# Vision tower on one core: the complex attention of the first half of the batch runs alone, the second half's runs under the first half's norms and first layer

## What is computed

```python
h = tokens(x)                                      # (8, 66, 192)
h = h + complex_attention(layernorm(h))
h = h + tower(layernorm(h))                        # 4 layers, RMS norms ln1, ln2, final

def complex_attention(x):                          # 12 heads of 16
    qr, qi, kr, ki, v = (heads(x @ W.T) for W in (Wqr, Wqi, Wkr, Wki, Wv))
    sr = (qr @ kr.T + qi @ ki.T) / 4
    si = (qi @ kr.T - qr @ ki.T) / 4
    return softmax(sqrt(sr * sr + si * si)) @ v

# one layer of the tower
nx = rms(h, ln1[i])
h = h + softmax(q @ k.T + bias) @ v @ attn_o[i]    # q, k, v = nx @ attn_q, attn_k, attn_v
nx = rms(h, ln2[i])
h = h + relu(nx @ ffn_wi[i]) @ ffn_wo[i]           # + experts in layers 1 and 3
```

## Time and profile before

| | us |
|---|---|
| runs | 795.41, 798.39, 814.34 |
| median of the runs | 798.39 |
| the profiled execution | 800.37 |
| its span from first to last instruction | 798.6 |

### The profile page before, as it was taken

One profiled execution on the slowest core, in us unless ns is written; L12 is line 12 of the kernel. 1 busy time (PEld: TensorE's weight loads), 2 busy tenths in 40 slices (PEclk: granted clock), 3 DMA queues, 4 the chain that ended last, 5 costly groups with the idle time before them and its releaser, 6 DMA issues.

```text
span 798.6 us, 16388 instructions
## 1 busy us (share of the span) xinstructions
PE 733.1 (92%) x6735; PEld 649.1 (81%) x6735; DVE 438.8 (55%) x917; ACT 406.8 (51%) x913; POOL 352.6 (44%) x327
## 2 busy tenths in 40 slices
PE   6887999998998989899999999989999899999995
PEld 4764577776877979899999887768779788999995
DVE  0338435365364484566666634753555845766664
ACT  1467335535354353377777355353553545766642
POOL 3346516463663440155766332536544413355420
PEclk9976899998998898999999999989999999999997
DMA  7221001021311201053445020012212011523300
GB/s 203 80 70 41 2 2 31 9 73 41 99 41 31 70 2 56 1 163 111 138 128 145 13 75 1 2 40 74 68 31 70 6 51 53 143 71 108 101 1 22
DMA packets 36610, 49.21 MB, mean 62 GB/s; under 512 B 6155, under 2 KB 27575, under 8 KB 36023
## 3 DMA queue, kind: packets, MB, share of 16 engines
q1 hardware_dynamic: 33259, 43.49, 18.8%
q10 hardware_dynamic: 3276, 4.67, 1.9%
HBM read 47.70 MB, written 0.45 MB: 60 GB/s over the span
## 4 chain that ended last, share of the span: by engine, by line
PE 65%; DVE 12%; ACT 11%; POOL 6%; issue 3%; DMA 2%; SPq 0%; POOLq 0%; ACTq 0%; DVEq 0%
PE pd L653 35%; PE pa L653 19%; PE ps L653 8%; POOL w L582 3%; PE pa L684 3%; ACT wide L1015 2%; POOL prob L591 1%; DVE prob L1208 1%; ACT pa L1016 1%; DVE rc L1060 1%; ACT wqkv L927 1%; DVE xn L1095 1%; DVE xs L1067 1%; DVE hT L1135 1%; DVE mx L1055 1%
## 5 line engine op out<-in xcount | busy, mean ns | idle before, releaser
L582 POOL TENSOR_TENSOR w<-raw,w 128x384 fp32r<-128x384 f32 x140 | 142.7, 1021 | 124.6 <-ACT w L927 116.7
L653 PE MATMUL pd<-wide,w 128*128 128x264 f32 x1200 | 159.7, 291 | 0.0
L653 PEld LDWEIGHTS pd<-wide,w 128*128 128x128 f32 x1200 | 153.6, 194 | 1.0 <-DVE wide L1231 0.5
L653 PE MATMUL pa<-xs,w 128*128 128x264 f32 x810 | 123.4, 293 | 10.5 <-DVE wide L1231 6.2
L653 PEld LDWEIGHTS pa<-xs,w 128*128 128x128 f32 x810 | 108.7, 193 | 16.0 <-DVE wide L1231 8.2
L591 POOL TENSOR_TENSOR prob<-prob,mx 66x792 f32<-66x792 f32 x36 | 54.9, 1528 | 75.4 <-DVE mx L1055 75.2
L1231 DVE TENSOR_TENSOR wide<-pa,wide 128x264 fp32r<-128x264 f32 x144 | 61.4, 430 | 33.6 <-ACT pa L1016 31.7
L653 PE MATMUL ps<-xs,w 128*128 128x264 f32 x480 | 74.4, 285 | 3.1 <-DVE prob L1208 3.1
L1015 ACT ACTIVATE wide<-pa 128x264 fp32r<-128x264 f32 x144 | 56.7, 394 | 33.3 <-PE pa L653 33.2
L597 POOL TENSOR_TENSOR prob<-prob,rc 66x792 f32<-66x792 f32 x36 | 54.3, 1509 | 36.7 <-DVE rc L1061 36.7
L603 POOL TENSOR_TENSOR rs<-var,exponent 88x3 f32<-88x3 f32 x22 | 18.6, 848 | 115.5 <-DVE var L1077 115.5
(11 more groups left out here) (125 smaller groups left out, 1240.7 us busy)
## 6 DMA issues: line engine op xcount, KB each, us to landing
raw<-in_moe_w_dram SPq DMA_DIRECT2D x16, 576.0 KB, 4.2
raw<-in_moe_w_dram SPq DMA_DIRECT2D x16, 384.0 KB, 3.5
raw<-in_moe_w_dram SPq DMA_DIRECT2D x32, 192.0 KB, 4.0
vtok<-cw_rows ACTq DMA_DIRECT2D x4, 1056.0 KB, 6.1
raw<-in_attn_o_dram SPq DMA_DIRECT2D x4, 576.0 KB, 4.0
raw<-in_ffn_wo_dram SPq DMA_DIRECT2D x4, 576.0 KB, 4.1
vtok<-in_patches_dram SPq DMA_DIRECT2D x2, 768.0 KB, 7.9
raw<-in_attn_q_dram SPq DMA_DIRECT2D x4, 384.0 KB, 3.6
```

Of the source, the lines that this page charges most:

```text
L582: ins = nc.gpsimd.tensor_tensor(low, whole, high.bitcast(F32), ALU.subtract)
L653: return nc.tensor.matmul(out_ap, lhsT, rhs, start=first, stop=last)
```

## The change

1. The list is written anew from the first `cproj` to the first `pv`. The weights q and k are split before and between the first half's projections. The first half's scores follow without the second half's projections between them, and its roots stand one by one between them. The second half's projections come after the first half's exponentials, its scores and roots under the first half's norms, and its exponentials, transposes, values and norms between the scores and values of layer 0 of the first half. `pv` of the first half's images 0 and 1 is drawn ahead of the second half's `qk`. The `warm` entries are placed anew: 41 matmuls stand from the first `cproj` to the second half's first `qk` where there were 77.
2. `croot` is a stage for one image instead of four, and `qk` a stage for q or k instead of both. What each computes is as before.
3. DVE's wait for the `ps` banks in `cscores` is counted from the list, since scores of layer 0 no longer come after all complex scores.

Everything from `o_tail` of layer 0 on is as it was.

```diff
@@ stages() @@
-    for part in range(3):
-        yield ("cproj", 0, part)
-        if part == 0:
-            yield ("scale", 1, "complex", 0)
     yield ("split", None, "qkv", 0, 0)
+    yield ("cproj", 0, 0)
+    yield ("scale", 1, "complex", 0)
     yield ("split", None, "qkv", 0, 1)
...
+    yield ("cscores", 0, 3)
+    yield ("croot", 0, 2)
+    yield ("croot", 0, 3)
+    yield ("cvals", 0)
+    yield ("cvals", 1)
...
+    yield ("cscores", 1, 3)
+    yield ("croot", 1, 0)
     yield ("norm", 0, "ln1", 0)
+    yield ("croot", 1, 1)
...
+                yield ("pv", 0, 0, 0)
+                yield ("scores_end", 0, 0)
                 yield ("split", None, "o", 0, 0)
+                yield ("scale", 1, "ln1", 0)
+                yield ("pv", 0, 0, 1)
+                yield from warm(6)
+                early = 2
...
@@ pool: croot @@
-                    for b in range(HALF_B):
-                        sub_max()
+                    sub_max()
@@ tensor: qk @@
-                    for i in range(2):
-                        pe.wait_ge(chunk_split, chunks_until("qkv", layer, i))
-                        for m in range(KT):
-                            product(bank_a()[:, 0:NT],
+                    if i == 0:
+                        pe.wait_ge(x_ready, x_ready_after(("scale", hf, "ln1", layer)))
+                        flush()
+                    pe.wait_ge(chunk_split, chunks_until("qkv", layer, i))
+                    for m in range(KT):
+                        product(bank_a()[:, 0:NT],
@@ scalar: croot @@
-                    for b in range(HALF_B):
-                        u = hf * HALF_B + b
-                        act.wait_ge(csq_free, 2 * (u + 1))
+                    u = hf * HALF_B + stage[2]
+                    act.wait_ge(csq_free, 2 * (u + 1))
@@ vector: cscores, croot @@
-                            dve.wait_ge(s_free, 2 * (u + 1))
+                            dve.wait_ge(s_free, groups_after(S_GROUPS, stage))
...
-                    for b in range(HALF_B):
-                        u = maxes.next() - 1
-                        dve.wait_ge(sqrt_ready, u + 1)
-                        max_of(u)
+                    u = maxes.next() - 1
+                    dve.wait_ge(sqrt_ready, u + 1)
+                    max_of(u)
```

More of the change, by code:

```diff
@@ L126, in stages @@
[L126 to L142, removed]
+    yield ("cexp", 0, 3)
+    yield ("cproj", 1, 0)
@@ new lines, in stages @@
+    yield from warm(12)
+    yield ("cproj", 1, 1)
+    yield ("ctp", 0, 0)
+    yield ("cproj", 1, 2)
+    yield ("cpv", 0, 0)
+    yield ("ctp", 0, 1)
+    yield from warm(3)
+    yield ("cpv", 0, 1)
+    yield ("ctp", 0, 2)
+    yield from warm(3)
+    yield ("cpv", 0, 2)
+    yield ("ctp", 0, 3)
+    yield ("split", None, "qkv", 0, 2)
+    yield from warm(3)
+    yield ("cpv", 0, 3)
+    yield ("cscores", 1, 0)
+    yield ("mean", 0, "encoder")
+    yield ("cscores", 1, 1)
+    yield ("squares", 0, "encoder")
@@ L143, in stages @@
+    yield ("norm", 0, "encoder", 0)
+    yield ("cscores", 1, 2)
+    yield from warm(2)
     yield ("scale", 0, "encoder", 0)
     yield ("squares", 0, "ln1")
-    yield from warm(2)
-    yield ("ctp", 1, 2)
-    yield from warm(2)
+    yield ("cscores", 1, 3)
+    yield ("croot", 1, 0)
     yield ("norm", 0, "ln1", 0)
[L149 to L153, removed]
-    yield ("scale", 0, "ln1", 0)
-    yield from warm(2)
@@ L161, in stages @@
         if layer not in MOE_LAYERS:
-            yield from warm(4)
-            yield ("qk", 0, layer)
             if layer == 0:
+                yield ("qk", 0, 0, 0)
+                yield ("cexp", 1, 2)
+                yield ("cexp", 1, 3)
+                yield ("qk", 0, 0, 1)
+                yield ("ctp", 1, 0)
+                yield ("scores", 0, 0, 0)
+                yield ("cpv", 1, 0)
+                yield ("ctp", 1, 1)
+                yield ("v", 0, 0, 0)
+                yield ("cpv", 1, 1)
@@ new lines, in stages @@
+                yield ("ctp", 1, 2)
+                yield ("scores", 0, 0, 1)
+                yield ("cpv", 1, 2)
+                yield ("ctp", 1, 3)
+                yield ("v", 0, 0, 1)
+                yield ("cpv", 1, 3)
+                yield ("mean", 1, "encoder")
+                yield ("scores", 0, 0, 2)
+                yield ("squares", 1, "encoder")
+                yield ("v", 0, 0, 2)
+                yield ("norm", 1, "encoder", 0)
+                yield ("scores", 0, 0, 3)
+                yield ("scale", 1, "encoder", 0)
@@ L165, in stages @@
+                yield ("squares", 1, "ln1")
+                yield ("v", 0, 0, 3)
+                yield ("norm", 1, "ln1", 0)
+                yield ("pv", 0, 0, 0)
+                yield ("scores_end", 0, 0)
                 yield ("split", None, "o", 0, 0)
-                yield ("mean", 1, "encoder")
-                yield ("squares", 1, "encoder")
-                beside = [[("norm", "encoder", 0)], [("scale", "encoder", 0), ("squares", "ln1")], [("norm", "ln1", 0)], [("scale", "ln1", 0)]]
-            else:
+                yield ("scale", 1, "ln1", 0)
@@ L170, in stages @@
+                yield ("pv", 0, 0, 1)
+                yield from warm(6)
+                early = 2
+            else:
+                yield from warm(4)
+                yield from qk(0, layer)
                 beside = [[("norm", "ln1", layer)], [("scale", "ln1", layer)], [], []]
-            for b in range(HALF_B):
[L172 to L176, removed]
@@ L177, in stages @@
-            yield ("qk", 1, layer)
+                for b in range(HALF_B):
+                    yield ("scores", 0, layer, b)
+                    for x in beside[b]:
+                        yield (x[0], 1) + x[1:]
+                    yield ("v", 0, layer, b)
+                yield from warm(6)
+                early = 0
+            yield from qk(1, layer)
             if layer == 0:
```

76 lines of the change are left out of this document (29 added, 47 removed).

## The result

The changed kernel takes 814.7 us in the median of four runs (813.0 to 816.2); the kernel before took 798.8 in the four beside them. The ratio on record is 1.0173 (the two medians give 1.020), with a 95% interval of 1.0132 to 1.0214: slower by 1.3 to 2.1%, where 0.8% faster was forecast. The profiled execution took 813.33 and spans 811.5, against 800.37 and 798.6.

What follows compares the result with a forecast made beforehand. The prediction took PE, busy 92% of the span, as the bound. Its stretches summed as 25.7 - 6.2 - 13.4 + 0.4 = 6.5 us earlier at `o_tail`, so 798.4 - 6.5 = 791.9 us, range 784 to 800.

Steps and rivals of the forecast that it cites:

- A: Stretch from 29.2 to the first half's fourth `cpv`: forecast to take 43.4 us, ending at 72.6 instead of 98.3.
- if the clock is back at about 53: Assumption for the first half's value products: the last three take 0.94 us each, ending at 56.4; range 55 to 58.
- B: Stretch from the first half's last `cpv` to its `qk`: forecast 23.2 us, 17.0 before, cutting the lead to 19.5.
- the wait behind the second half's root: First half's ln1 `var` and power queue behind the second half's image 0: 4.5 us given away.
- C: Stretch from the first half's `qk` to the second half's: forecast 42.3 us, 28.9 before, cutting the lead to 6.1.
- If the 2.7 us of idle time before 138.1 bring it down: Bound on PE's clock at the second half's `qk`: it could lose up to about 4 us, leaving a lead of 2.5.
- rival 3: Clock falls before the second half's `qk` (4 us), later waits 2 us longer, no lead left: 797.9 us; chance 0.15.
- D: Stretch from the second half's `qk` to `o_tail`: forecast 31.3 us, 31.7 before.
- PE arrives 3.5 too early: Before `o_tail`, PE waits 3.5 us for ACT's copies of `v` behind POOL's weight split, where it waited 1.2 before.
- the lead of 6.5: Forecast gain at `o_tail` summed over the four stretches: 6.5 us earlier than before, at 169.4.
- All that follows shifts by it: From `o_tail` on, unchanged work was to move by the 6.5 us gained, giving 791.9 us.
- Rival 2: PE leaves the sparse norm stretch at 1.2 GHz and following work runs at half rate: 806.9 us; chance 0.10.

Runs made afterwards that it cites:

- e14: e9 with the second half's first projection moved ahead of the first half's value products: 790.3 us, ratio 0.9851.
- e1: The changed kernel with the first half's ln1 norm moved ahead of the second half's first root: 811.4 us, ratio 1.0122.
- e3: The changed kernel with the split of w1 moved ahead of the second half's first `qk`: 802.0 us, ratio 0.9987.
- e8: The kernel before with the split of w1 moved ahead of the second half's `qk`: 799.3 us, ratio 0.9987.
- e2: The changed kernel with 32 more filler matmuls between and behind the first half's complex scores: 812.3 us, ratio 1.0138.
- e11: The changed kernel with 11 more `warm` around the encoder norm and 6 ahead of its second-half scale: 810.4 us, ratio 1.0108.
- e4: The kernel before with 37 `warm` put ahead of layer 0's `o_tail` as a pure delay: 809.4 us, ratio 1.0077.
- e12: The changed kernel measured again, unedited: 815.0 us, ratio 1.0174.
- e10: e9 with the filler around the first half's encoder norm added: 793.6 us, ratio 0.9881.
- e13: The kernel before with the early split of w1 and 36 more filler matmuls: 797.1 us, ratio 0.9955.
- e9: The changed kernel with e1, e2, e3 and e6 combined, filler placed ahead of the second half's norm scales, `pv` of image 1 moved back: 794.5 us, ratio 0.9894.
- e15: e9 measured again, unchanged: 794.0 us, ratio 0.9910.
- e6: The changed kernel with the second half's ln1 scale moved ahead of the first `pv` and layer 0's last sum: 812.4 us, ratio 1.0164.

## Why the prediction was wrong, step by step

**A, "if the clock is back at about 53": failed.** Of the 6.6 us, 4.1 are the clock's: the last five value products took 8.4 instead of 6.3, and the rest of the stretch 18.2 instead of 16.2. The clock's return was taken from the earlier trace rows, 9 and 11 us after PE took up work again; here it took 21 us (from 44.8 to 65.8, and 24 from the fall). The step had this as a point with a range of 2 us; its bounds were too narrow. (The prediction has the falls "some 1.5 to 2 us" after PE ran out of work; by the windows of the same trace it was 1.0 and 2.0, and 3.4 at the third.) The other 2.5 us are the later start of the fourth value product, and most of that a term that the sum left out: ACT's last root waited 1.51 for DVE's additions beside POOL, which the prediction counted in B and not in A. e14 ends within 0.6 of the forecast, but with other work in this wait, so it doesn't show that the work was replayed rightly.

**B, the wait behind the second half's root: there, and about half as dear.** Expected to give away 4.5 us, it delayed PE's spread by 3.3 of idle time; e1 without it shortened B by 2.1. From the table load to `qk` it was 9.8 where 10.0 was forecast; the load itself came 14.6 after A's end where 13.2 was forecast.

**C: order right, clock wrong.** The prediction started `qk` cold, with the clock back at 100. It came back at 103.3, just ahead of `qk` at 103.6, so `qk` ran at full rate and took 8.4 instead of 9.8. The rest of C lost 3.6: the clock fell at 134, 1.8 us after PE's wait of 1.40 for POOL's power, and stayed down until 151. "If the 2.7 us of idle time before 138.1 bring it down" was the bound of this step, and rival 3 priced it with 4 us; it should have been in the forecast. In the trace of before a gap of 1.33 had left the clock alone, and from that one case I took that such gaps do.

**D, "PE arrives 3.5 too early": held to 0.3 us, and priced wrongly.** POOL's first subtraction was forecast 17.6 after `qk` and came at 18.1, ACT's copies at 20.5 and came at 20.4, PE's wait at 3.5 and was 3.80. The sum had this wait as idle time only, so D came out 0.4 shorter than before; it was 4.0 longer. It left out what the earlier trace rows show beside such gaps, the clock's fall: 10 us at half rate, 4.4 us in the stretch. e3, without the wait, took 8.3 less in D and 12.7 less in the whole; e8 shows that the same split cost nothing that can be measured before, where PE came later.

No single step turned the sign. A alone used up the lead of 6.5; without D's 4.4 `o_tail` would still be 3.5 later than before. But D is the step whose removal by one moved stage (e3) brought the kernel back to the time of before. That the clock, and not the waits alone, carries much of the loss is read from the traces (68 us at 0.50 against 31); e2 and e11, which only add filler, gain 2 to 5 us by the medians and don't resolve it.

**"All that follows shifts by it": right on average, by e4; what else is lost behind `o_tail` is open.** The ratio stands for about 14 us, and `o_tail` is 7.9 late (7.4 in e12); the rest is behind it, where the work is the same. From `o_tail` to PE's end the traces of before and after take 618.2 and 623.2, with 10 and 12 spells of slow clock; but e12, the changed kernel again, takes 620.3, and over all traces of this case the stretch takes between 615.9 (e3) and 626.9 (e10), with e13, an edit of the kernel before, at 623.6. One trace of each kernel can't tell 5 us there from chance, and why the medians differ by more than `o_tail` does isn't shown.

**The rivals.** Rival 2, "the clock eats it: slower", names what happened, but put it in B and C, as 30 us of work at half rate, and gave it 0.10. It happened as four spells, in A, B, C and D. Rival 3 had the clock in C and D's waits 2 longer; it needed D's clock too. Much of the error is this: one cause behind all steps was counted as independent small bounds, and all of them came out to the same side.

**The table loads** took 1.28 each as forecast. The Trainium skill (ScalarE: Activation LUTs, "What ACT_TABLE_LOAD costs") adds 1.38 for a drain. The trace doesn't agree: the load at 93.77 begins 0.02 after ACT's squares end, and the roots start 0.01 after the load's end (95.06), so there is no room for one on either side.

## What to carry to other kernels

When a stretch is reordered so that PE arrives earlier at an unchanged producer, the new wait costs its own length and then, if the clock falls, half of all work until it returns. Here 3.8 us of waiting and 10 us of slow clock behind it went with 8.3 us of D, by e3. So look first at what another queue (here POOL with 7.4 us of weight split) has in front of the operation that PE will need, and move that along with the rest. Real work from later in the list can fill a gap that is left: the projections in e14 closed the wait that the filler around it in e9 had left open.

## What the runs showed of the hardware

**A slow clock can outlast full work by far.** In after PE is busy without a break from 52.6 on, and but for 0.65 us from 44.8, with matmuls that take twice their time, and the clock is back only in the window at 65. The stretch from 52.6 is all value products of 128x192, then three projections, then filler; the return comes in the filler, 4.8 us after the first projection. In e14's trace PE was busy in every microsecond from 149 to 175 and had 0.50 throughout.

**The same gap doesn't always bring it down.** e15 and e14 have the same list from here on. Windows of 1 us, of e15, then of e14:

```profile
149.00:150.00 1.00, 0.38 (x7) 1.00 0.46 68
150.00:151.00 1.00, 0.92 (x14) 1.00 0.86 304
```

```profile
145.00:146.00 1.00, 0.28 (x5) 1.00 0.52 104
146.00:147.00 1.00, 0.92 (x14) 1.00 0.91 338
...
148.00:149.00 1.00, 1.00 (x5) 0.66 0.41 108
```

Both wait for ACT's copy of `v`, 0.70 and 0.80 us. In one the clock stays at 1.00; in the other it is at 0.50 for the next 27 us and `o_tail` comes 39.1 after `qk` instead of 29.0. The wait of 1.23 in D did nothing in the trace of before and cost the clock for 17 us in e4's. In these traces gaps of 0.7 to 1.4 us sometimes bring the clock down and sometimes don't, and those of 2.69 (ahead of 85.19 in B) and 3.80 did. The Trainium skill (TensorE: Matmul & The Clock Gate, "HAM oscillation — how this bites in real kernels") tells of a kernel whose waits of some 3 to 5 us for DMAs bring the clock down every time; the trace agrees for the 3.80 here, and the shorter gaps are the ones that differ from one execution to the next. This may be much of the 10 us of scatter, which no run tests, and it is why a gap of about 1 us should be counted as a risk and not as its own length.

**DVE beside POOL.** The two subtractions of x's split take 1.11 and 1.13 us beside POOL's operations on two tensors (after) and 0.43 each away from them (e6).
